# Storing the first sixteen tokens of b and of the last x tile by themselves, and letting the first round's loads wait for these alone

## The reference, cut to what matters

```python
x = x + attention(x)
xr, gate = split(x @ W_in.T);  xc = silu(conv(xr + t_emb));  xn = layernorm(xc) * ln_g + ln_b
Bm, Cm, dt = split(xn @ W_xproj.T);  Ad = 1 - 0.01 * tanh(dt @ W_dt.T + b_dt) * tanh(A_log)
Bd = Bm * min(norm(xn), 1)
def step(h, (ad, bd, xt, ct)):                       # scanned over 256 tokens
    h = clip(h * ad[:, :, None] + bd[:, :, None] * xt[:, None, :], -10, 10)
    return h, einsum('bd,bdh->bh', ct, h)
x = x + ((y + D * xn) * silu(gate)) @ W_out.T
```

## Time and profile before

| what | value |
|---|---|
| time, median of 3 runs (lowest to highest) | 562.97 us (562.87 to 564.33) |
| time of the profiled execution | 563.17 us |
| its span, first to last instruction | 561.4 us |
| busy shares of the span | PE 84%, DVE 77%, PEld 50%, ACT 45%, POOL 35% |
| mean granted TensorE clock | 0.948 |

### The profile page before, as it was taken

The page is one execution under the profiler, slowest core; times in us unless marked ns, Lnnn a source line. Parts: engine busy times, 40 slices in busy tenths (PEclk is TensorE's granted clock), DMA queues, the critical chain, the costliest instruction groups (busy, mean ns, idle before and its releaser), DMA issues.

```text
span 561.4 us, 8412 instructions
## 1 busy us (share of the span) xinstructions
PE 471.6 (84%) x3000; PEld 281.7 (50%) x3000; DVE 430.0 (77%) x744; ACT 253.5 (45%) x504; POOL 194.0 (35%) x211
## 2 busy tenths in 40 slices
PE   1958897999999979888999820889999999999996
PEld 1844565667676656567888610123333333333333
DVE  2846353766857676849998982999999999999993
ACT  3322675777576635778667664043221111111111
POOL 6405303023031100000730694079873443343332
PEclk9967898999999999999999875799999999999999
DMA  8884576765847540100065266676545444333310
GB/s 335 320 166 87 85 145 120 139 123 102 166 95 151 112 97 1 39 27 12 0 251 173 94 224 119 205 227 207 189 128 111 127 121 126 121 112 100 100 37 20
DMA packets 44629, 71.80 MB, mean 128 GB/s; under 512 B 18825, under 2 KB 33545, under 8 KB 41468
## 3 DMA queue, kind: packets, MB, share of 16 engines
q1 hardware_dynamic: 40684, 67.55, 45.9%
q0 software_dynamic: 528, 3.55, 1.6%
q10 hardware_dynamic: 3376, 0.16, 0.3%
HBM read 41.88 MB, written 23.02 MB: 116 GB/s over the span
## 4 chain that ended last, share of the span: by engine, by line
PE 49%; DVE 32%; DMA 7%; ACT 5%; issue 4%; POOL 2%; SPq 1%; DVEq 0%; POOLq 0%
DVE win L1664 10%; PE bank L1320 6%; PE bank L1280 6%; PE bank L1291 5%; PE bank L963 5%; PE bank L993 5%; PE bank L940 5%; DVE z L1664 5%; DMA qst<-mT 5%; PE bank L978 4%; PE bank L1042 2%; DVE acc L1464 2%; DVE zlast L1664 2%; DVE lnb_rep L1664 2%; PE bank L1011 2%
## 5 line engine op out<-in xcount | busy, mean ns | idle before, releaser
L1486 DVE TENSOR_REDUCE mx<-bank 128x2 f32<-128x512 f32 x128 | 82.0, 686 | 70.8 <-PE bank L963 70.2
L1280 PE MATMUL bank<-xst,bst 128*128 128x512 bf16 x256 | 82.8, 394 | 39.1 <-DMA bst<-bd_d 23.2
L693 ACT ACTIVATE ex<-bank 128x512 f32<-128x512 f32 x128 | 70.9, 599 | 43.1 <-PE bank L978 43.1
L1664 DVE CUSTOM_DVE_ANT_0 win<-win,bank,hi 128x512 f32<-128x512 f32 x96 | 71.8, 748 | 3.4
L1280 PEld LDWEIGHTS bank<-xst,bst 128*128 128x128 bf16 x256 | 24.9, 98 | 92.8 <-DVE win L1664 30.7
L455 POOL TENSOR_TENSOR qk<-qk,part 128x512 f32<-128x512 f32 x16 | 19.7, 1231 | 128.3 <-ACT part L618 128.3
L978 PE MATMUL bank<-qst,kst 97*128 97x256 bf16 x256 | 46.1, 273 | 10.0 <-DMA qst<-mT 8.3
L963 PE MATMUL bank<-kst,qst 96*128 96x256 bf16 x256 | 49.6, 288 | 5.5 <-DVE mx L1486 5.5
L940 PE MATMUL bank<-xnT,w 128*128 128x256 f32 x192 | 51.9, 428 | 0.8 <-ACT xnT L603 0.7
L563 POOL TENSOR_TENSOR yg<-yT,gateT 128x128 f32<-128x128 f32 x60 | 29.3, 521 | 60.1 <-ACT yT L873 60.1
L865 ACT ACTIVATE ytk<-bank,ybias 128x512 f32<-128x512 f32 x15 | 10.3, 687 | 84.5 <-PE bank L1291 84.5
(11 more groups left out here) (190 smaller groups left out, 906.4 us busy)
## 6 DMA issues: line engine op xcount, KB each, us to landing
qk_d<-part SPq DMA_DIRECT2D x64, 96.0 KB, 2.5
xs_d<-xpart SPq DMA_DIRECT2D x16, 384.0 KB, 4.7
xst<-xs_d SPq DMA_DIRECT2D x15, 384.0 KB
xn_d<-xc SPq DMA_DIRECT2D x16, 256.0 KB, 3.3
xtk<-xn_d SPq DMA_DIRECT2D x64, 64.0 KB
xst<-xs_d SPq DMA_DIRECT2D x15, 256.0 KB
bd_d<-zeros POOLq DMA_DIRECT2D x1, 3468.0 KB, 12.1
qst<-qk_d SPq DMA_DIRECT2D x8, 384.0 KB, 4.5
```

The source lines that it names most:

```text
L693: nc.scalar.activation(ex[:, n // 4, n % 4, :], bank[6 + n % 2][:, :], ACT.Exp, scale=SCALE)\
L1280: mm(bank[t % 4][:, :], bst[:, slot, t % RS, :], xst[slot][:, t % RS, :], start=True, stop=True)\
L1486: v.tensor_reduce(mx[:, :, STACKED[n]:STACKED[n] + 1], bank[4 + n % 2][:, :].rearrange("p (t k) -> p t k", t=HALVES), AX.X, ALU.max)\
L1664: v._custom_dve(bass.dve_ops.TENSOR_ADD_SAT, out=zst[t % ZR], in0=zst[(t - 1) % ZR], in1=bank[t % 4][:, :], s0=hi[:, t:t + 1], s1=0.0).the ...
```

## The change

1. `store_b`, `store_parts` and `store_d` take a range of tokens and a semaphore's name.
2. When `bsplit` comes, SP and ACT store only tokens 0 to 15 of b (three transfers each, 128 pieces of 32 bytes each), on a new semaphore `bd_first`, which the `dpart` store counts on too. SP then stores only tokens 0 to 15 of tile 7, on a new semaphore `xs_first`.
3. The first round's `load_x` waits for tiles 0 to 6 and `xs_first`; its `load_b` for `bd_first` (seven transfers).
4. The rest of tile 7 (tokens 16 to 127) is stored by SP behind the first round's loads, and SP waits for it ahead of round 1's `load_x`. The rest of b (six transfers of 896 pieces) is issued by ACT alone, behind its four activations; SP waits for it (`bd_out0`) ahead of round 1's `load_b`.
5. ACT waits for `xs_first` too before it reuses tile 7's slot of the ring (j = 12).

```diff
-        def store_b(eng, t, which):
+        def store_b(eng, t, which, lo=0, hi=P, done=None):
...
-                eng.dma_start(rows[t * P:(t + 1) * P], bpart[:, PAIRS[j][1], t, :].rearrange("p (b d) -> p b d", b=B))\
-                   .then_inc(s[f"bd_out{t}"], 16)
+                eng.dma_start(rows[t * P + lo:t * P + hi],
+                              bpart[lo:hi, PAIRS[j][1], t, :].rearrange("p (b d) -> p b d", b=B))\
+                   .then_inc(s[done or f"bd_out{t}"], 16)
...
-            def store_parts(j):
+            def store_parts(j, lo=0, hi=P, done=None):
...
-                sp.dma_start(xs_d[:, b, t * P:(t + 1) * P, :].rearrange("k p c -> p k c"), xpart[:, j % XRING, :, :])\
-                  .then_inc(s[f"xs_out{j % XRING}"], 16)
+                sp.dma_start(xs_d[:, b, t * P + lo:t * P + hi, :].rearrange("k p c -> p k c"),
+                             xpart[lo:hi, j % XRING, :, :]).then_inc(s[done or f"xs_out{j % XRING}"], 16)
...
-            store_d(0)
+            store_d(0, "bd_first")
             store_xn(B - 2)
             store_parts(B - 2)
             store_xn(B - 1)
             sp.wait_ge(s["bsplit"], 1)
-            store_b(sp, 0, range(3))
-            store_parts(B - 1)
-            parts_stored(B)
+            store_b(sp, 0, range(3), 0, RS, "bd_first")
+            store_parts(B - 1, 0, RS, "xs_first")
+            parts_stored(B - 1)
+            sp.wait_ge(s["xs_first"], 16)
             load_x(0, "ld_xf", 0, FIRST)
-            sp.wait_ge(s["bd_out0"], 16 * 7)
+            sp.wait_ge(s["bd_first"], 16 * 7)
             load_b(0, "ld_bf", 0, FIRST)
             load_x(0, "ld_x0", FIRST)
             load_b(0, "ld_b0", FIRST)
+            store_parts(B - 1, RS, P)
             sp.wait_ge(s["ones_in"], 16)
+            parts_stored(B)
             load_x(1, "ld_x1")
+            sp.wait_ge(s["bd_out0"], 16 * 6)
             load_b(1, "ld_b1")
...
+                if j == B - 1 + XRING:
+                    act.wait_ge(s["xs_first"], 16)
...
             act.wait_ge(s["bsplit"], 1)
-            store_b(act, 0, range(3, 6))
+            store_b(act, 0, range(3, 6), 0, RS, "bd_first")
             act.wait_ge(s["shift_ready"], 1)
             for j in range(IN_FRONT, NT):
...
+            store_b(act, 0, range(6), RS, P)
             act.wait_ge(s["ybias_ready"], 1)
```

More of the change, by code:

```diff
@@ L248, in build @@
             parts_ready xs_out0 xs_out1 xs_out2 xs_out3 xs_out4 ones_in xn_norm xn_late zfill shift_ready dx_ready xn_out0 xn_out1 nrm_ready nrm1_ready dt_in dt_out eb_ready eb_tr ipc_ready eb_back
-            dsplit bsplit bsplit1 ipct_ready bd_out0 bd_out1 c_ready ld_xf ld_bf ld_x0 ld_b0 ld_x1 ld_b1 u_done z_ready
+            dsplit bd_first xs_first bsplit bsplit1 ipct_ready bd_out0 bd_out1 c_ready ld_xf ld_bf ld_x0 ld_b0 ld_x1 ld_b1 u_done z_ready
             y_done y_taken cst_ready ld_xt0 ld_xt1 ysum_ready yt_done yg_ready yt_taken
@@ L362, in load_b, with store_d @@
                                  rows[:, i * RS + lo:i * RS + hi, :]).then_inc(s[name], 16)
-            def store_d(t):
+            def store_d(t, done):
                 rows = bd_d[24 * BP:27 * BP].rearrange("(k t c) -> t k c", k=3, c=P)
-                sp.dma_start(rows[t * P:(t + 1) * P], dpart[:, :, t, :]).then_inc(s[f"bd_out{t}"], 16)
+                sp.dma_start(rows[t * P:(t + 1) * P], dpart[:, :, t, :]).then_inc(s[done], 16)
             def load_xn(r):
@@ L422, in _ @@
                     sp.wait_ge(s["bsplit1"], 1)
-                    store_d(1)
+                    store_d(1, "bd_out1")
                     store_b(sp, 1, range(6))
```

## The result

The changed kernel takes 560.65 us (median of 20 runs), the kernel before 564.52 beside it (20 runs). The ratio is 0.9931, with a 95% interval from 0.9909 to 0.9953: faster by 3.9 us (2.7 to 5.1). Single executions of the kernel before lie between 560.28 and 568.18 us, so the size of each part has to be read in the trace, from one fixed event to another. I use **L**, the time from the end of b's last part on VectorE to VectorE's first step of the recurrence. Before it is 350.53 - 335.62 = 14.91 us.

What follows compares the result with a forecast made beforehand. VectorE's chain of 256 steps was taken as the bound, its start held up by the stores: 4.5 us earlier less 0.4 for overlap gives 4.1, so 562.97 becomes 558.9 us, range 557.4 to 561.3.

Steps and rivals of the forecast that it cites:

- What bounds the kernel: From 350.53 us on, VectorE's chain of 256 steps at 0.785 us; moving its first step moves the end equally.
- Issue of the b stores: SP's three b stores ahead of tile 7: 1.5 us to issue instead of 3.49, bounds 1.2 to 1.8.
- Landing of tile 7's first rows: Store ahead of `load_x`: lands in 2.3 us instead of 4.80, bounds 1.8 to 3.3; `load_x` 4.5 us earlier.
- The b stores' own landing costs nothing: Wait ahead of the first `load_b`: b stores land by 340.3 at the latest, needed only at 341.8.
- The rest of b beside the loads: ACT's six late stores run during round 0's first loads: costs 0.4 us, bounds 0 and 2.4.
- Rival A: The rest of b delays round 0's first loads by all 2.4 us: gain 2.1, time 560.9; chance 0.13.
- ACT's own delay: ACT's parts of tiles 8 and 9 start some 3.8 us later, hidden by its 20.36 us of idle time.
- The Trainium skill's rule: At the first loads, semaphores would wait for small writes ahead of them; overlap cost above zero, unconfirmed by the trace.
- Round 1 and what follows: New waits take nothing back: slack shrinks from 5.3 to 2.9 us; `xtk` loads some 1.8 earlier, POOL 3 ahead.
- The clock and the 0.5 us stall: Round 0: TensorE's first 9 us at a granted clock of 0.50 and the 0.5 us short wait both stay.
- Rival B: Tile 7's first rows still take about 4.8 us to land: gain 1.6, time 561.4; chance 0.06.
- Rival C: Waiting for the rest of b ahead of round 1's `load_b` becomes the bound: slower, 576 if served serially; chance 0.03.

Runs made afterwards that it cites:

- later-rest experiment: Changed kernel, but ACT issues the rest of b only once the first piece of round 0 has landed; 560.90 us, ratio 0.9907 to the kernel before.
- tile 7 first: Changed kernel with tile 7's first sixteen rows stored ahead of SP's three b stores; ratios 0.9882 and 0.9921 to the kernel before.
- 64 tokens: Changed kernel with 64 tokens of b and tile 7 stored first instead of 16; 563.11 us, one execution timed.

## Why the prediction was right, step by step

It said 558.9 with a gain of 4.1 us; measured are 3.9 (2.7 to 5.1) by the times and 4.24 by the profile. The 560.65 is 1.75 above the 558.9: 1.55 of it since the kernel before, run beside it, stood at 564.52 and not at the 562.97 of three runs, and 0.2 is gain that was missing by the times. The mechanism was right; that the sum came out to 0.1 us of the profile is partly luck, since an error of 0.3 us in the issue and one of 0.3 in the overlap cancel.

- *What bounds the kernel*: right. First to last step 200.21 and 200.22 us, and where a wait was put into it the time grew by just that.
- *Issue of the b stores*, 1.5 us: measured 1.82, because they took 0.55, 0.70 and 0.45 (bounds 1.2 to 1.8). 0.3 too little.
- *Landing of tile 7's first rows*, 2.3: measured 2.23, of which 0.3 is ACT's stores beside it, which the prediction had put at the loads. `load_x` begins 4.17 us after b's end, forecast 3.93, before 8.47: 4.3 earlier, not 4.5.
- *The b stores' own landing costs nothing*: right. In the changed kernel SP went from `load_x` (ended at 344.01) to `load_b` (344.05) without a wait.
- *The rest of b beside the loads*, 0.4: the size was right, the place was not. The loads lost 0.06, since 6.50 stands against 6.44. The 0.4 of the later-rest experiment sits in the landing of tile 7's rows, because ACT issues its stores between its activations and not after them: from 1.9 us after b's end, where 4.6 was forecast. Without it that landing would have been 1.9. Rival A is a matter of timing: with tile 7 first it cost the loads 0.55.
- *ACT's own delay*, 3.8 us hidden by its idle time: there was none (5.40 and 5.43 us after b's end), and the six stores took 3.4 us to issue, not 4.6. The assumption behind it, that stores wait for the activations ahead of them in the program, was wrong; its price is the 0.3 us in the landing above.
- *The Trainium skill's rule* (DMA: Bandwidth & Descriptors, Queues, rings and completion order), that a semaphore's increment waits for earlier writes of its DMA engine across queues: the 1.0 us that ACT's stores added to tile 7's whole store on the other queue agrees with it in direction. Sharing of the engines would do the same, and no run here tells the two apart.
- *Round 1 and what follows*: nothing was given back, as said, but tile 7's rest took 3.0 to land and not 2.6, so that 2.1 us of slack were left where 2.9 were forecast; the `xtk` loads, forecast 1.8 us earlier, came 1.0 earlier when counted from b's end (364.07 - 337.65 = 26.4 against 363.04 - 335.62 = 27.4), and POOL was ready 2.2 us ahead of need instead of 3.
- *The clock and the 0.5 us stall* in round 0: unchanged in the change, as said. Over the other kernels the stall was between nothing (64 tokens) and 0.51 us.
- *Rival B* did not come: 2.23 and not 4.8. *Rival C* did not come in the change, but its mechanism is real: with the rest of b later still, VectorE waited 4.96 us at its seventeenth step and first to last took 5.47 us more. In another kernel the same wait held up SP's list behind it and cost 0.43 us one round later.

## What to carry to other kernels

When a transfer on the critical path is late to land, count the pieces in front of it, not the bytes: taking 5376 pieces of 32 bytes (168 KB) off the path was worth 2.5 us by itself, taking 336 KB of tile 7 off it 0.65. Bytes are not free, though: once b's pieces were gone, the same 336 KB were worth 1.74, and a gain measured for one cut depends on whether the other is made. Pieces of another size were not tried. Store first what the next consumer needs, put the rest where an engine idles, and then check two moments: what the rest lies beside, and which later wait it has become. Read a gain of 4 us from one event to the next within a trace; between whole executions of this kernel the part ahead of it moved by as much.

## What the runs showed of the hardware that was not expected

- ACT issued transfers while its activations were still running. The first activation started at 339.46 and the first of the six stores behind all four activations in the program at 339.57.
- Small pieces on one queue slow a transfer on the other: tile 7's 384 KB landed in 3.88 us beside ACT's stores and in 2.89 without them, its 48 KB in 2.23 and 1.91.
- How long issuing takes depends on what else is under way: the same six stores took ACT 3.4 us to issue in the changed kernel, 3.9 to 4.3 in the kernels with tile 7 first and with only b split, and 5.0 to 6.3 us in the five where they were held back and issued beside the loads of the second piece or of round 1.
